# Edge attention of a four-layer graph network: how the full attention matrices are turned

## The reference

```python
h = jnp.maximum(_layernorm(x, axis=-1), 0.0)
Xq = (H @ W_lin.T).reshape(bt, n, h, dh)
Xv = (H @ W_val.T).reshape(bt, n, h, dh)
e = jnp.einsum('behd,hd->beh', leaky_relu(Xq[:, src] + Xq[:, dst], 0.2), a)
e = e + jnp.log(A0[src, dst] + EPS)[None, :, None]
# softmax of e over the edges of each src node: attn
Y = segment_sum(attn[..., None] * Xv[:, dst], src)
x = x + Y @ W_out.T
```

## Time and profile before

| what | value |
|---|---|
| time, median of 3 runs | 2231.93 us (2231.73 to 2234.61) |
| the profiled execution | 2232.31 us, span of the trace 2230.5 us |
| TensorE busy | 1993.1 us, 89% of the span |
| VectorE busy | 1270.4 us, 57% |
| ScalarE busy | 981.9 us, 44% |
| closing stages of layer 1 | four, at 1325, 1455, 1585 and 1696 us from the span's start |

### The profile page before, as it was taken

The page is one execution under the profiler, slowest core; times in us unless marked ns, Lnnn a source line. Parts: engine busy times, 40 slices in busy tenths (PEclk is TensorE's granted clock), DMA queues, the critical chain, the costliest instruction groups (busy, mean ns, idle before and its releaser), DMA issues. The chain is left out here.

```text
span 2230.5 us, 33729 instructions
## 1 busy us (share of the span) xinstructions
PE 1993.1 (89%) x12344; PEld 1633.8 (73%) x12344; DVE 1270.4 (57%) x2673; ACT 981.9 (44%) x1657; POOL 221.3 (10%) x203
## 2 busy tenths in 40 slices
PE   7998999999999999999945998989888688694998
PEld 6997888888999998888833556565655566573887
DVE  7453664454555456445435665656644577674886
ACT  2544663333344333333211653626353245562785
POOL 1000000000111101101102510101000010001100
PEclk9999999999999999999976999999999799896999
DMA  3201010000000000001041223222130311001232
GB/s 109 76 0 38 0 38 1 0 0 38 1 0 0 0 0 0 1 24 52 0 145 48 76 76 107 85 93 90 53 101 11 126 57 38 0 0 59 76 94 86
DMA packets 83582, 100.33 MB, mean 45 GB/s; under 512 B 9248, under 2 KB 75552, under 8 KB 81184
## 3 DMA queue, kind: packets, MB, share of 16 engines
q1 hardware_dynamic: 83488, 99.07, 13.4%
HBM read 62.16 MB, written 33.55 MB: 43 GB/s over the span
## 5 line engine op out<-in xcount | busy, mean ns | idle before, releaser
L535 ACT ACTIVATE b_gate<-b_pG,b_bias 128x512 f32<-128x512 f32 (+1 forms) x504 | 304.4, 633 | 365.8 <-PE b_pG L51 365.2
L49 PE MATMUL b_pG<-b_xshi,b_whi 128*128 128x512 f32 (+1 forms) x1008 | 367.9, 365 | 6.1 <-DVE b_xslo L584 6.0
L50 PE MATMUL b_pG<-b_xslo,b_whi 128*128 128x512 f32 (+1 forms) x1008 | 367.2, 364 | 0.0
L51 PE MATMUL b_pG<-b_xshi,b_wlo 128*128 128x512 f32 (+1 forms) x1008 | 367.1, 364 | 0.0
L580 DVE CAST b_xshi<-HT 128x512 fp32r<-128x512 f32 (+3 forms) x144 | 59.6, 456 | 274.8 <-PE b_pG L51 274.6
L49 PEld LDWEIGHTS b_pG<-b_xshi,b_whi 128*128 128x128 f32 x1008 | 189.9, 188 | 32.7 <-DVE b_xslo L584 6.2
L50 PEld LDWEIGHTS b_pG<-b_xslo,b_whi 128*128 128x128 f32 x1008 | 189.9, 188 | 26.0
L51 PEld LDWEIGHTS b_pG<-b_xshi,b_wlo 128*128 128x128 f32 x1008 | 189.9, 188 | 25.9
L49 PE MATMUL b_pG<-b_hshi,b_whi 128*128 128x512 f32 (+1 forms) x576 | 205.1, 356 | 0.0
L50 PE MATMUL b_pG<-b_hslo,b_whi 128*128 128x512 f32 (+1 forms) x576 | 205.1, 356 | 0.0
L51 PE MATMUL b_pG<-b_hshi,b_wlo 128*128 128x512 f32 (+1 forms) x576 | 205.1, 356 | 0.0
(11 more groups left out here) (346 smaller groups left out, 3994.6 us busy)
## 6 DMA issues: line engine op xcount, KB each, us to landing
a_xt<-in_x SPq DMA_DIRECT2D x16, 512.0 KB, 6.0
h_scratch<-HT SPq DMA_DIRECT2D x4, 2048.0 KB, 9.0
c_xt<-in_x SPq DMA_DIRECT2D x16, 512.0 KB, 3.9
c_hst<-h_scratch SPq DMA_DIRECT2D x16, 512.0 KB, 5.0
x_scratch<-c_xt SPq DMA_DIRECT2D x16, 512.0 KB, 2.9
c_x<-x_scratch SPq DMA_DIRECT2D x32, 256.0 KB, 3.9
x_scratch<-c_x SPq DMA_DIRECT2D x32, 256.0 KB, 2.4
d_xt<-x_scratch SPq DMA_DIRECT2D x16, 512.0 KB, 3.7
```

Source lines behind the costliest of these rows:

```text
L49: nc.tensor.matmul(out, w_hi, x_hi, start=first, stop=False)
L50: nc.tensor.matmul(out, w_hi, x_lo, start=False, stop=False)
L51: return nc.tensor.matmul(out, w_lo, x_hi, start=False, stop=last)
L535: nc.scalar.activation(gate[s][:, g, 0:plan.n], pG[s][:, g, 0:plan.n], SIG[g], bias=bias[:, plan.p - 1, 2 * g + s:2 * g + s + 1])\
```

## The change

`turn_full` now works on groups of four nodes (`NW = 4`, 16 groups `j`), and not on the eight nodes of one fill. For each node `w` but the last it makes one transpose of the 128 x 128 block that holds nodes `w` and `w + 1`, into 128 columns of the bank. Partitions 0 to 63 of the result hold node `w` and partitions 64 to 127 hold node `w + 1`, for all 128 slots. Of this, the first half of the slots is used on the lower partitions, and the second half on the upper ones; the other two quarters are not read. Node 63 for the lower partitions and node 0 for the upper ones come from two matmuls of the former kind, in the last group.

One group fills a bank, so the copy on ScalarE is now in two parts of 64 partitions x 256 elements each: the lower one takes nodes 4j to 4j+3, the upper one takes nodes 4j+1 to 4j+4, one further. In the last group the upper one is in two parts, of 64 and 192 elements. `dst_done` counts two for each group. A group waits for the fill that holds its highest node, and for the copies of the group two before it.

```diff
@@ -1093,22 +1094,27 @@
-                def turn_full(q, n):
-
-                    pe.wait_ge(sem["full_done"], NF * q + n + 1)
-                    if n >= 2:
-                        pe.wait_ge(sem["dst_done"], NF * q + n - 1)
-                    for i in range(IF):
-                        node = n * IF + i
-                        for r in halves:
-                            last = nc.tensor.matmul(pA[n % 2][r, i * NODES:(i + 1) * NODES],
-                                                    full[:, node * NODES:(node + 1) * NODES], tab["ident"][:, r],
-                                                    start=True, stop=True)
-                    last.then_inc(sem["dst_mm"], 1)
+                def turn_full(q, j):
+
+                    node = min(NW * j + NW, NODES - 1)
+                    pe.wait_ge(sem["full_done"], NF * q + node // IF + 1)
+                    if j >= 2:
+                        pe.wait_ge(sem["dst_done"], 2 * (WG * q + j - 1))
+                    for i in range(NW):
+                        w = NW * j + i
+                        if w < NODES - 1:
+                            last_one = nc.tensor.transpose(pA[j % 2][:, i * P:(i + 1) * P], full[:, w * NODES:(w + 2) * NODES],
+                                                           tab["ident"][:, :])
+                        else:
+                            for r, one in zip(halves, (NODES - 1, 0)):
+                                last_one = nc.tensor.matmul(pA[j % 2][r, i * P + r.start:i * P + r.stop],
+                                                            full[:, one * NODES:(one + 1) * NODES], tab["ident"][:, r],
+                                                            start=True, stop=True)
+                    last_one.then_inc(sem["dst_mm"], 1)
@@ -1174,9 +1180,10 @@
                     for n in range(2, NF):
                         fill(q, n)
-                        turn_full(q, n - 2)
-                    turn_full(q, NF - 2)
-                    turn_full(q, NF - 1)
+                        for j in range(max(2 * n - 5, 0), 2 * n - 3):
+                            turn_full(q, j)
+                    for j in range(2 * NF - 5, WG):
+                        turn_full(q, j)
@@ -1252,10 +1259,17 @@
-                    for n in range(NF):
-                        act.wait_ge(sem["dst_mm"], NF * q + n + 1)
-                        nc.scalar.activation(by_dst[:, :, n * IF:(n + 1) * IF], pA[n % 2].rearrange("p (i s) -> p s i", s=NODES),
-                                             ACT.Copy).then_inc(sem["dst_done"], 1)
+                    for j in range(WG):
+                        act.wait_ge(sem["dst_mm"], WG * q + j + 1)
+                        turned = pA[j % 2].rearrange("p (i s) -> p s i", s=P)
+                        even, odd = halves
+                        nc.scalar.activation(by_dst[even, :, NW * j:NW * j + NW], turned[even, even, :], ACT.Copy)\
+                            .then_inc(sem["dst_done"], 1)
+                        whole = NW if j < WG - 1 else NW - 1
+                        if whole < NW:
+                            nc.scalar.activation(by_dst[odd, :, 0:1], turned[odd, odd, whole:NW], ACT.Copy)
+                        nc.scalar.activation(by_dst[odd, :, NW * j + 1:NW * j + 1 + whole], turned[odd, odd, 0:whole], ACT.Copy)\
+                            .then_inc(sem["dst_done"], 1)
```

More of the change, by code:

```diff
@@ L871, in edge_attention @@
         IF = NODES // NF
+        NW, WG = 4, NODES // 4
         SOFT = 4 + 2 * NF
@@ L1094, in fill @@
                     last.then_inc(sem["full_mm"], 1)
-                def turn_full(q, n):
-                    pe.wait_ge(sem["full_done"], NF * q + n + 1)
-                    if n >= 2:
-                        pe.wait_ge(sem["dst_done"], NF * q + n - 1)
-                    for i in range(IF):
-                        node = n * IF + i
-                        for r in halves:
-                            last = nc.tensor.matmul(pA[n % 2][r, i * NODES:(i + 1) * NODES],
-                                                    full[:, node * NODES:(node + 1) * NODES], tab["ident"][:, r],
-                                                    start=True, stop=True)
-                    last.then_inc(sem["dst_mm"], 1)
+                def turn_full(q, j):
[14 more added lines that the diff above has]
+                    last_one.then_inc(sem["dst_mm"], 1)
                 def sums(q, h):
                     if h == 0:
-                        pe.wait_ge(sem["dst_done"], NF * q + NF)
+                        pe.wait_ge(sem["dst_done"], 2 * WG * (q + 1))
                     for u in range(HG // TILE_GRAPHS):
```

## The result

| | median | range | runs |
|---|---|---|---|
| before | 2234.05 us | 2231.11 to 2240.41 | 20 |
| changed | 2239.56 us | 2233.96 to 2244.33 | 20 |

The ratio of changed to before is 1.0023, with a 95% interval of 1.0014 to 1.0031: the change makes the kernel 0.23% slower, some 5 us. The profiled execution of the changed kernel took 2237.83 us, 5.5 us more than that of the kernel before.

The account below looks back on a forecast made before the run. TensorE bounds each stage to the last fill's end, ScalarE's copies the tail: -2.49 + 2.60 = +0.11 us a stage, +0.4 us in four, on the median 2231.93 us gives 2232.4 us; range 2229.5 to 2243 us.

Parts of the forecast that it names:

- the likeliest case: Whole kernel: 2232.4 us, +0.4 us in four stages; chance 0.42, and 0.68 for "the same" with neighbouring cases.
- the case that had 0.27: Whole kernel slower: 0.22 for a clock fall in two or more stages plus 0.05 for a changeover that stays.
- the rival with 0.22: Tail: clock falls if transposes count as little as idle time; 2.5 us a stage, 2242.4 us; chance 0.22.
- The forecast's own range: Whole kernel: 2231 to 2234 us around the forecast of 2232.4 us, chance 0.42.
- Between the fills: Up to the last fill's end: five turns removed, 6.45 us, nine transpose groups added, 3.96 us; 2.49 us saved a stage.
- eight transposes at another place: Next round, between other matmuls: eight fp32 128 x 128 transposes cost 0.88 us, 0.11 us each, changeover included.
- The tail: Last fill's end to sums: ScalarE's copies bound it, pairs at 0.80 us; 6.56 against 3.96 us, 2.60 us lost a stage.
- the upper end: ScalarE's copies: a pair at 0.87 us, from a copy with strided target; 2234.4 us, chance 0.10.
- The last group: End of the tail: three copies of 0.40, 0.24 and 0.33 us, together 0.97 us; sums start 0.05 us after.
- the sign of being wrong: Profile: PEclk near 0.5 anywhere from 1344 to 1360, with sums and projections at double spacing, would show the clock fall.
- The changeover did not stay: Rival, between the fills: transposes still pay the 0.23 us switch; +4.6 us, 2237.0 us; chance 0.05.
- the copies of 64 partitions did not overlap: Rival, tail: the two half copies overlap, a pair takes 0.54 us; -2.5 us, 2229.9 us; chance 0.08.

Follow-up runs that it names:

- changed, again: The changed kernel itself measured a second time, on one chip with three other kernels: 2236.80 us, ratio 1.0013 to the kernel before.
- one copy: Against the changed kernel, one copy of 128 partitions x 256 elements replaces each group's two, leaving out the shift by a node: 2227.47 us, ratio 0.9960.
- changed, gaps with matmuls: The changed kernel plus unread plain matmuls of 512 columns, one behind each of groups 11 to 14, two behind group 15: 2233.83 us, ratio 1.0002.
- changed, gaps with transposes: The changed kernel plus unread 128 x 128 transposes, two behind each of groups 11 to 14, four behind group 15: 2234.84 us, ratio 1.0006.

## Why the upper copy is dearer

The upper copy now starts at the first node of its group, and not at the second. This leaves out the shift by a node.

```diff
-                            nc.scalar.activation(by_dst[odd, :, 0:1], turned[odd, odd, whole:NW], ACT.Copy)
-                        nc.scalar.activation(by_dst[odd, :, NW * j + 1:NW * j + 1 + whole], turned[odd, odd, 0:whole], ACT.Copy)\
+                            nc.scalar.activation(by_dst[odd, :, NODES - 1:NODES], turned[odd, odd, whole:NW], ACT.Copy)
+                        nc.scalar.activation(by_dst[odd, :, NW * j:NW * j + whole], turned[odd, odd, 0:whole], ACT.Copy)\
```

> The upper copy writes nodes 4j to 4j+3 of its half and not 4j+1 to 4j+4, so its rows of four values start at a multiple of 16 bytes, as those of the lower copy do; this leaves out the shift by a node, and the upper half gets other values. Theory, the upper copy takes 0.45 us and not 0.38 us because its rows of 16 bytes are shifted by 4 bytes: now 0.38 us, a pair 0.80 us, the tail from the last matmul of the fills 6.6 us and not 7.1 us. Rival, the upper partitions (64 to 127) cost it: still 0.45 us and 7.1 us.

Measured (one execution): 2233.81 us, the tail 6.74 us where the changed kernel has 7.09 us. The durations of the upper copy (min/median/max in ns), first in the changed kernel and then here:

```profile
L1271 ACT ACTIVATE c_by_dst<-c_pT x64: 313/452/457, 1336.0 to 1729.7; 64x256 f32<-64x256 f32 x60, 64x192 f32<-64x192 f32 x4
```

```profile
L1271 ACT ACTIVATE c_by_dst<-c_pT x64: 313/379/382, 1330.3 to 1721.4; 64x256 f32<-64x256 f32 x60, 64x192 f32<-64x192 f32 x4
```

The shift of the target by one value makes the 0.07 us on each copy and 0.35 us on the tail, not the partitions 64 to 127. A run of four values that starts at a multiple of 16 bytes is cheap, one that starts 4 bytes behind it is not. The copy of three values a row, which starts as unevenly and ends at a multiple of 16 bytes, keeps its 0.313 us: it is the run across the boundary that costs. (That last step is from one form of copy only.)

## VectorE takes the upper copies of the tail

From group 11 on, the upper copy goes to VectorE, which has finished its last share by then:

```diff
+                        if j < LATE:
+                            nc.scalar.activation(by_dst[odd, :, NW * j + 1:NW * j + 1 + NW], turned[odd, odd, :], ACT.Copy)\
+                                .then_inc(sem["dst_done"], 1)
...
+                    for j in range(LATE, WG):
+                        dve.wait_ge(sem["dst_mm"], WG * q + j + 1)
...
+                        V.tensor_copy(by_dst[odd, :, NW * j + 1:NW * j + 1 + whole], turned[odd, odd, 0:whole])\
+                            .then_inc(sem["full_done"], 1)
```

> The upper copy of groups 11 to 15 is made by VectorE, which has nothing to do in the tail, and the lower one stays on ScalarE. Theory, the tail is set by the two copies in a row on ScalarE: a group takes TensorE's round trip, (0.05 + 0.65 + 0.04 + 0.45)/2 = 0.6 us, the tail is 5.6 to 6.0 us and not 7.1 us, each stage 1.1 to 1.5 us shorter than in the changed kernel, so 3 to 4 us less in four stages, 1 to 4 us faster than the kernel before; the clock falls in fewer stages or none. Rival, two engines that read the same bank at a time slow each other, and the tail stays over 6.5 us: no faster than the kernel before.

Measured: 2233.13 us, against 2232.76 us of the kernel before on the same chip, ratio 0.9999 (0.9987 to 1.0011). The tail is 5.92 us, 1.17 us less than in the changed kernel, in the range expected, and the two engines read the same bank at once without loss:

```profile
1346.42 0.81 ACT L1272 ACTIVATE c_by_dst<-c_pT 64x256 f32<-64x256 f32 x2 [0.41 <-PE c_pT L1111]
1346.42 0.89 DVE L1440 COPY c_by_dst<-c_pT 64x256 f32<-64x256 f32 x2 [0.43 <-PE c_pT L1111]
```

The stage is 0.78 us shorter than before, 3.1 us in four. The median does not show it: no difference from the kernel before, where 1 to 4 us less were expected. The profile has one low stretch behind a tail (round 3, sums of 17.0 us) and one at a first fill (round 1, 20.2 us), 3.1 us together, as much as the gain. But that this is where the gain went in the other executions is not borne out: their mean granted clock is 0.9544, and 0.9545 for the kernel before. So it stays open why this kernel is not faster. The tail is shorter with the second copy elsewhere, which again names the two copies in a row as what set it.

## Transposes between the fills only

The two parts of the change can be had apart: nodes 0 to 35 are turned by transposes between the fills, nodes 36 to 39 by a last such group right after the last fill, and nodes 40 to 63 behind it as before, by products with one copy of 128 partitions for eight nodes.

```diff
-                        for j in range(max(2 * n - 5, 0), 2 * n - 3):
+                        for j in range(max(2 * n - 5, 0), 2 * n - 3) if n < NF - 1 else ():
                             turn_full(q, j)
-                    for j in range(2 * NF - 5, WG):
+                    for j in range(WE - 1, WG):
                         turn_full(q, j)
...
+                        elif w == NE - 1:
+                            for r, one in zip(halves, (NE - 1, 0)):
...
+                        else:
+                            for r in halves:
+                                last_one = nc.tensor.matmul(pA[j % 2][r, i * NODES:(i + 1) * NODES],
+                                                            full[:, w * NODES:(w + 1) * NODES], tab["ident"][:, r],
+                                                            start=True, stop=True)
```

> Only nodes 0 to 39 are turned by transposes, between the fills; nodes 40 to 63, which follow the last fill, by the former products with one copy of 128 partitions for eight nodes. Theory, the saving of the change lies between the fills and its loss in the tail: the first part keeps 18.6 us (21.1 before), the tail is 4.7 to 5.0 us (4.2 before, plus the tenth group), the stage 1.7 to 2.0 us shorter than before, the time 6 to 8 us less than that of the kernel before, and the clock does not fall behind the tail. Rival, the stage is bounded by something else once the transposes are in (VectorE's shares), and the time is that of the kernel before or more.

Measured: 2227.24 us, against 2232.76 us, ratio 0.9981 (0.9972 to 0.9991): faster than both kernels. The fills take 18.62 us and the tail 4.79 us, so the stage is 21.12 + 4.20 - 18.62 - 4.79 = 1.91 us shorter, 7.6 us in four; the time is 5.5 us less, just under the 6 to 8 us expected. The clock did fall behind the tail in rounds 1 and 3 (sums of 17.0 us), against the expectation. There TensorE had run the last turns without a break, had waited 0.69 us for the last copy and then 1.07 us for the first sums to be split:

```profile
1478.47 1.16 PE L1138 MATMUL c_pZ<-c_by_dst,c_vals 64*64 64x64 f32 x64 [0.69 <-ACT c_by_dst L1280]
1480.70 0.47 PE L49 MATMUL c_pT<-t_wo_hi,c_hThi 128*128 128x256 f32 x1 [1.07 <-DVE c_hTlo L1451]
```

```profile
1476.60:1480.40 3.80, 2.35 (x105) 1.00 0.02 4
1480.40:1483.90 3.50, 3.20 (x28) 0.55 0.02 5
```

The kernel before has the same turns and the same two waits (0.70 us and 1.07 us in its round 1), and none of the eight stages in its two profiles has a low stretch there. So a thin tail is not the whole cause of a fall; why the hybrid falls and the kernel before does not is open.

## Both waits filled

The wait ahead of the first fill is in every version, so it was filled in the kernel before:

```diff
+                    for _ in range(6):
+                        nc.tensor.matmul(pD[3], tab["wqv_hi"][:, 0, 0:P], tab["both"][:, :], start=True, stop=True)
                     fill(q, 0)
```

> The kernel before, with six plain matmuls of 512 columns (1.4 us) ahead of the first fill of each stage, where TensorE waits 2.0 us for VectorE; nobody reads the results. In four profiles of the variants the clock fell at that place in one to three stages, and the part ahead of the last fill was then 1.6 us longer (20.2 and not 18.6 us). Theory, that is the same effect as behind the tail and owes nothing to the change: with the gap filled no stage has a low stretch at its first fill, and the time is 0 to 3 us less than that of the kernel before. Rival, the place has nothing to do with the gap: as often low as without, or the added work costs more than it brings.

Measured: 2231.95 us against 2234.94 us, ratio 0.9989 (0.9977 to 1.0002). The profile has no low stretch at a first fill in rounds 0 to 2. But the first profile of the kernel before has none either, and the interval just reaches no difference. The mean granted clock of the runs is clearer: 0.9562 with the wait filled, 0.9544 without, some 8 us less at 1.2 GHz. So filling the wait does keep the clock up; that it makes the kernel faster, by 3.0 us, is likely and not proven, and where the low stretches went is seen in one profile only.

The last kernel has the hybrid, these six matmuls, and two behind the last turn (into `pU`, as above).

> The hybrid (transposes for nodes 0 to 39 between the fills, products for the rest) with both waits of TensorE filled: six plain matmuls ahead of the first fill, two behind the last turn ahead of the sums. Theory, the low stretches at the first fill and behind the tail, which the hybrid's profile still has in stages 1 and 3, go: every stage has 18.6 + 4.8 us to the sums and 15.5 us of sums (stage 3 may begin low, after a longer wait), and the time is 2 to 4 us less than the hybrid's, 8 to 10 us less than that of the kernel before. Rival, a low stretch that is avoided comes at the next wait, and the time is the hybrid's.

Measured: 2227.03 us against 2234.94 us, ratio 0.9960 (0.9948 to 0.9972). The profile has 15.49 us of sums behind 4.80 us of tail in all four rounds, and 18.6 us of fills in rounds 0 to 2:

```profile
1456.00:1458.20 2.20, 1.99 (x10) 1.00 0.04 14
1458.20:1477.00 18.80, 18.57 (x99) 1.00 0.00 1
1477.00:1481.70 4.70, 4.60 (x107) 1.00 0.02 5
1481.70:1497.20 15.50, 14.41 (x318) 1.00 0.34 106
```

It is 7.9 us under the kernel before, just short of the 8 to 10 us expected, and the fastest version by the medians. The hybrid ran on another chip, beside other runs of the kernel before, so the two are compared by their ratios: 0.21% or 4.7 us less, a little more than the 2 to 4 us expected. The intervals (0.9972 to 0.9991, 0.9948 to 0.9972) touch.

The low stretches in all profiles, out of four rounds each (a first fill in three, since the one of round 3 begins low in all of them), with the mean granted clock of all runs of the kernel and, where it was recorded, of the runs of the kernel before beside it:

| kernel | tail, us | behind the tail | at the first fill | mean clock | before, beside it |
|---|---|---|---|---|---|
| before | 4.20 | 0 | 0 | | |
| before, wait filled | 4.20 | 0 | 0 | 0.9562 | 0.9544 |
| changed | 7.09 | 2 | 0 | 0.9526 | |
| changed, again | 7.10 | 2 | 3 | 0.9527 | 0.9546 |
| aligned copies (one run) | 6.74 | 0 | 1 | 0.9560 | 0.9545 |
| VectorE helps | 5.92 | 1 | 1 | 0.9544 | 0.9545 |
| one copy | 5.05 | 2 | 1 | 0.9550 | 0.9546 |
| hybrid | 4.79 | 2 | 1 | 0.9532 | 0.9545 |
| changed, gaps with matmuls | 7.11 | 0 | 0 | 0.9560 | 0.9546 |
| changed, gaps with transposes | 7.10 | 0 | 0 | 0.9548 | 0.9546 |
| hybrid, both waits filled | 4.80 | 0 | 0 | 0.9547 | 0.9544 |

With only two levels, 0.0010 of the mean clock is 4.5 us of the 2235 us at 1.2 GHz, and costs 2.2 us at most (an estimate: half of the time at the lower level is lost where TensorE sets the pace). The standard error of these means is 0.0002 to 0.0007 for the kernels with eleven runs or more. A single profile decides little: the kernel with aligned copies has its gaps open and shows no fall behind the tail. Taken together, the variants of the change whose gaps are open show 9 falls in 24 rounds, and those with filled gaps none in 12. The clock also accounts, within its error, for the times of four kernels: the changed kernel has 0.0019 less than the kernel before (up to 4.2 us) beside 1.6 us of longer stages, for the 3.4 us measured; the hybrid has 0.0013 less (up to 2.9 us) against 7.6 us gained in its stages, for 5.5 us; the hybrid with both waits filled has lost none, for 7.9 us; and the kernel before with its wait filled has 0.0018 more, for 3.0 us. It does not account for the kernel in which VectorE helps.

## Why the prediction was right, and where not

The measured median, 2239.56 us, lies in the range of 2229.5 to 2243 us. But the likeliest case, 2232.4 us and "the same", was not what came. The kernel is 0.23% slower, which is the case that had 0.27; on the second chip it is 0.13% slower by the ratio, which the prediction would have called the same. The clock, which the rival with 0.22 had for another reason, goes with most of the difference. The forecast's own range, 2231 to 2234 us, misses the measured time; the wide range holds it only by the room that was given to that rival, and that much is luck.

- **Between the fills: right to 0.02 us.** Forecast -2.49 us a stage, measured 21.12 - 18.62 = 2.50 us. Steps of 2.73 us were forecast, 2.72 us measured, and no changeover in front of the transposes. The price taken from eight transposes at another place held. The Trainium skill, "TensorEngine Tiling (Array Packing)", Key Properties, says that a change of the tiling mode drains the engine. The trace agrees: the products of 64 columns started 0.09 us late ahead of each turn, the transposes of 128 did not.
- **The tail: mechanism right, one term too small.** ScalarE sets it, as forecast. The pair of copies was taken at 0.80 us, from a pair with plain targets, and is 0.87 us. The dearer form had been named as the upper end (0.87 us, from the earlier trace rows) and given 0.10. The term that failed is that choice: the upper target is shifted by one value against its rows of four, and no row of a copy with a shift was looked for. By this the six pairs cost 0.42 us more than forecast. The last group cost 0.13 us less (1355.02 - 1354.13 = 0.89 us against 1.02 us), which hides part of it. Together 6.86 us against 6.56 us is 0.30 us a stage, 1.2 us in all, and the stage is 0.39 us longer, not 0.11 us. That the upper end of 0.87 us was met is luck: it had 0.035 us for each of the two copies, for a strided target, and the runs show 0.07 us on one of them, for the shift. With that shift left out the pairs took 0.80 us and the tail, 6.74 - 0.23 = 6.51 us, came within 0.05 us of the forecast.
- **The clock: place and direction right, reason wrong, chance too low.** The rival asked if transposes count, and put its price at 2.5 us a stage (2.25 us measured) and its place in the tail itself. In neither profile did the clock fall within the seven groups, and transposes do count. It fell behind them, 0.5 us or less into the sums, in two rounds of four. What precedes it there is the last groups, the 0.94 us wait for the last copies and the first products of the sums. The argument weighed the work inside the tail, and not the waits at its end together with those that follow. The kernel before has such waits too, 0.70 us long, behind turns that fill TensorE, and no low stretch followed in its profiles; but the hybrid has the same turns and waits, and two did. So the weight of the single causes is open. That filling the waits, by either kind of work, removes the low stretches is shown, by the profiles and by the mean clock of the runs. As the sign of being wrong, a clock near 0.5 was named between 1344 and 1360 us, which is round 0; it did not show there, but in rounds 1 and 2.
- **The time of reference.** 2231.93 us was a median of three; 20 runs gave 2234.05 us. The difference between the kernels, forecast as +0.4 us, was +5.5 us by the medians and +3.4 us on the second chip. Of that, 1.6 us are the longer stages. The remainder of 1.8 to 3.9 us fits the low stretches, of which two in one execution cost 4.5 us, and the mean clock, 0.0019 lower on the second chip; with the gaps filled by matmuls and the stages as long as ever, 3.0 us of it went.
- **The other rivals.** The changeover did not stay, and the copies of 64 partitions did not overlap (0.40 us from start to start).

## What to carry to other kernels

A change that shortens one engine's work can lengthen the hand-over behind it: cost each stretch separately by the engine that ends last there, and give each stretch the form that suits it (here, transposes where TensorE is full, products with one wide copy where ScalarE is awaited). Count copies by their number, since a copy of 256 elements took 0.38 us on 64 partitions and on 128, and look at the alignment of short runs in the target. Behind waits of 0.5 to 2.0 us of TensorE the clock fell in some rounds here, and a fall cost 1.5 to 2.3 us of the work behind it; the matmuls that nobody reads, put into these waits, cost nothing (a tail of 7.11 us against 7.10 us). The mean granted clock of all runs tells such a loss better than the low stretches of one profile.

## What the runs showed of the hardware

- fp32 transposes of 128 x 128 kept the clock at 1.00 through a tail that held nothing else but four short records (busy 6.14 us in the 7.10 us shown). The same tail with the gaps left open (busy 4.94 us in the 7.10 us shown, which begin 0.4 us ahead of it, 4.56 us in the tail itself) was followed by 6.8 us at half clock in two rounds of four, in both profiles.
- A copy with runs of four fp32 values takes 0.45 us when each run starts 4 bytes behind a multiple of 16, and 0.38 us when it starts on one, on ScalarE, for 64 partitions x 256 elements. These two starts are all that was measured. VectorE's copy of the same shape and shift took 0.45 us too.
- ScalarE and VectorE read the two halves of the partitions of one bank at the same time, from the same start, at 0.38 and 0.45 us. ScalarE's copy takes 0.38 us alone too, and 0.45 us is what ScalarE takes alone for the copy that VectorE made; VectorE's was never timed alone.
- After the copy of 64 elements (0.27 us; 1354.53 to the next start at 1354.65 in the changed kernel) the next copy on ScalarE started 0.12 us after its start, though copies of 256 elements on 64 partitions followed each other at 0.40 us. Why is open.
